# Latent attention: four reciprocals of a head become one, and the four scalings wait once

## What is computed

```python
kv_lat = xn @ W_kvd
q_lat = xn @ W_qd
k = (kv_lat @ W_ku).reshape(B, S, NH, HH)
q = (q_lat @ W_qu).reshape(B, S, NH, HH)
v = (kv_lat @ W_vu).reshape(B, S, NH, HD)
...
scores = jnp.einsum('bqhd,bkhd->bhqk', qq, kk) * scale
causal = jnp.tril(jnp.ones((S, S), dtype=bool))
scores = jnp.where(causal[None, None], scores, jnp.finfo(scores.dtype).min)
probs = jax.nn.softmax(scores, axis=-1)
y = jnp.einsum('bhqk,bkhd->bqhd', probs, v).reshape(B, S, H)
return y @ W_o
```

## Time and profile before

| what | us |
|---|---|
| median of 3 runs | 2147.19 |
| the three runs | 2139.01 to 2148.48 |
| the profiled execution | 2150.66 |
| its span, first to last instruction | 2148.7 |
| TensorE busy | 1624.5 (76%) |
| VectorE busy | 1142.2 (53%) |
| ScalarE busy | 543.6 (25%) |
| GpSimd busy | 537.0 (25%) |
| mean granted TensorE clock | 0.884 |

### The profile page before, as it was taken

The page is one execution under the profiler, slowest core; times in us unless marked ns, Lnnn a source line. Parts: engine busy times, 40 slices in busy tenths (PEclk is TensorE's granted clock), DMA queues, the critical chain, the costliest instruction groups (busy, mean ns, idle before and its releaser), DMA issues. The chain is left out here.

```text
span 2148.7 us, 34575 instructions
## 1 busy us (share of the span) xinstructions
PE 1624.5 (76%) x10302; PEld 1283.0 (60%) x10302; DVE 1142.2 (53%) x2756; ACT 543.6 (25%) x1372; POOL 537.0 (25%) x763
## 2 busy tenths in 40 slices
PE   3994999998169776877774887527898698499980
PEld 2873888887159733444442576515565486398980
DVE  5774222221866667777764223365787676422223
ACT  1441011010144323666631100022221344011100
POOL 1002111111610013667722133240222100222215
PEclk8996999999589988999996989955999799699995
DMA  3103889886300017534201288720000000599973
GB/s 114 33 0 114 299 294 305 296 297 212 89 1 0 0 61 135 79 55 63 39 1 54 70 239 264 215 67 1 0 0 0 0 0 0 170 320 305 324 254 117
DMA packets 182251, 262.65 MB, mean 122 GB/s; under 512 B 17616, under 2 KB 132752, under 8 KB 180144
## 3 DMA queue, kind: packets, MB, share of 16 engines
q1 hardware_dynamic: 171968, 234.01, 36.3%
q0 software_dynamic: 10224, 27.93, 5.0%
HBM read 231.86 MB, written 30.02 MB: 122 GB/s over the span
## 5 line engine op out<-in xcount | busy, mean ns | idle before, releaser
L1026 POOL TENSOR_TENSOR xn<-xn,l1a_rc 128x512 f32<-128x512 f32 (+3 forms) x256 | 176.1, 719 | 92.2 <-DVE l1a_rc L958 92.2
L988 ACT ACTIVATE xn<-l1a_sc,l1a_nm 128x512 f32<-128x512 f32 (+3 forms) x256 | 131.4, 525 | 88.2 <-DVE l1a_nm L952 88.2
L1081 PE MATMUL l1a_tp<-consts,xn 128*128 128x128 f32 x640 | 87.5, 287 | 45.1 <-POOL xn L1026 22.5
L1622 PE MATMUL e0b_gp<-e0b_xT,e0b_wgu 128*128 128x128 f32 x936 | 117.2, 283 | 2.5 <-DVE e0b_hT L1691 1.3
L1622 PEld LDWEIGHTS e0b_gp<-e0b_xT,e0b_wgu 128*128 128x128 f32 x936 | 109.8, 195 | 15.4 <-issue 12.3
L1206 POOL DMA_INDIRECT e_got<-y_slots,e_slot x96 | 99.9, 1041 | 75.3 <-issue 73.0
L1643 PE MATMUL e0b_yp<-e0b_wd,e0b_hT 128*128 128x256 f32 x468 | 115.1, 388 | 0.6 <-issue 0.6
L952 DVE TENSOR_REDUCE l1a_nm<-l1a_sc 128x1 f32<-128x512 f32 (+3 forms) x256 | 107.1, 480 | 4.6 <-PE l1a_sc L1069 4.4
L1672 ACT ACTIVATE e0b_sg<-e0b_gp 128x640 f32<-128x640 f32 x78 | 33.5, 481 | 286.8 <-PE e0b_gp L1622 286.8
L1081 PEld LDWEIGHTS l1a_tp<-consts,xn 128*128 128x128 f32 x640 | 73.7, 147 | 52.3 <-POOL xn L1026 51.4
L536 PE MATMUL a_sc<-a_kd,a_qT 128*128 (+2 forms) x256 | 99.5, 523 | 4.4 <-ACT a_qT L609 2.9
(11 more groups left out here) (477 smaller groups left out, 3551.3 us busy)
## 6 DMA issues: line engine op xcount, KB each, us to landing
e3b_wgu<-in_L_ffn_W SPq DMA_DIRECT2D x78, 512.0 KB
e0b_wgu<-in_L_ffn_gate_proj SPq DMA_DIRECT2D x39, 704.0 KB
e0b_wgu<-in_L_ffn_up_proj SPq DMA_DIRECT2D x39, 704.0 KB
e0b_wd<-in_L_ffn_down_proj SPq DMA_DIRECT2D x39, 640.0 KB
e3b_wd<-in_L_ffn_W SPq DMA_DIRECT2D x39, 512.0 KB
e1b_wgu<-in_L_ffn_Wg_r SPq DMA_DIRECT2D x39, 256.0 KB
e1b_wgu<-in_L_ffn_Wu_r SPq DMA_DIRECT2D x39, 256.0 KB
e1b_wd<-in_L_ffn_Wd_r SPq DMA_DIRECT2D x39, 256.0 KB
```

The lines of the kernel that those rows point to most:

```text
L988: nc.scalar.activation(pr[:, j, of_query[q]], sc[q][:, 0:(q + 1) * P], ACT.Exp, bias=nm[:, q:q + 1], accum_out=sums[:, j, q:q + 1]).then_i ...
L1026: nc.gpsimd.tensor_tensor(of, of, bcast(rc[:, j, q:q + 1], 2, (q + 1) * P), ALU.mult)\
L1081: last = nc.tensor.transpose(tp[g][:, q - k + (TB - 2 if k == TB - 1 else 0), :], pr[:, j, at:at + P], ident)
L1622: last = nc.tensor.matmul(dst[:, f, :], wgu[j][:, k, at + f * P:at + (f + 1) * P], xT[j][:, k, :], start=(k == 0), stop=(k == KC - 1))
```

## The change

`invert` becomes one instruction: it waits until the last of the head's four exponentials is done and takes the reciprocals of all four columns of sums, 128x4, at once. It adds 1 to `rec_done` in place of four times 1. `scale` waits once, for the head's reciprocal, and then issues the same four multiplications in the same order, which still add 1 to `scaled` each. Nothing else differs.

```diff
@@ -953,9 +953,8 @@
                         def invert(n, j):
-                            for m, q in enumerate(reversed(range(TB))):
-                                dve.wait_ge(exp_done, n * TB + m + 1)
-                                nc.vector.reciprocal(rc[:, j, q:q + 1], sums[:, j, q:q + 1]).then_inc(rec_done, 1)
+                            dve.wait_ge(exp_done, n * TB + TB)
+                            nc.vector.reciprocal(rc[:, j, :], sums[:, j, :]).then_inc(rec_done, 1)
@@ -1020,8 +1019,8 @@
                         def scale(n, j):
-                            for m, q in enumerate(reversed(range(TB))):
-                                pool.wait_ge(rec_done, n * TB + m + 1)
+                            pool.wait_ge(rec_done, n + 1)
+                            for q in reversed(range(TB)):
                                 of = pr[:, j, of_query[q]].unsqueeze(1)
                                 nc.gpsimd.tensor_tensor(of, of, bcast(rc[:, j, q:q + 1], 2, (q + 1) * P), ALU.mult)\
                                     .then_inc(scaled, 1)
```

## The result

| | before | changed |
|---|---|---|
| median, us | 2144.74 (9 runs) | 2156.61 (9 runs) |
| lowest to highest | 2135.27 to 2148.48 | 2151.32 to 2168.22 |
| ratio to before | 1 | 1.0071, 95% interval 1.0047 to 1.0095 |
| span of the profiled execution | 2148.7 | 2165.9 |

What follows compares the result with a forecast made beforehand. The prediction took a VectorE-ScalarE loop without slack as the bound. Terms 12.0 + 0.3 + 0.9 + 0.8 + 0.3 = 14.3 us on the 2147.19 median gave 2161.5, forecast as 2161 us (chance 0.63), range 2151 to 2170.

Steps and rivals of the forecast that it cites:

- The ring: In the 64-head attention, VectorE and ScalarE wait on each other in a loop without slack, 3.94 us a head.
- a place of no slack every fourth head: On TensorE, value products follow the turn and delay the next scores; 15 places where a later turn costs time.
- The last scaling gates the turn: TensorE's turn of a head's ten blocks would wait for GpSimd's last scaling and end 0.86 us later (0.79 to 0.99).
- The longer reciprocal: On VectorE, 128x4 takes 0.018 us more ahead of the copies in 48 heads, 0.9 us in all (0 to 4.4).
- three instructions fewer: On VectorE, removing three reciprocals a head gains nothing, as they ran in gaps ended by waits for ScalarE.
- The last head: At the attention's end, the last value products start at 1098.58 in place of 1097.75, costing 0.8 us.
- The first head: At the attention's start, it fills an empty pipeline and can lose 0 to 0.86 us; 0.3 taken.
- The place at a low clock: One of 15 places before value products, TensorE's granted clock 0.69, turn 2.23 us; cost taken as 0.3 us (0 to 0.86).
- The sum: All losses in the attention stage together: 12.0 + 0.3 + 0.9 + 0.8 + 0.3 = 14.3 us.
- the first rival: GpSimd's later scalings don't gate TensorE's turn: 4.5 to 9.4 us slower, 2152 to 2157, some 2155 us; chance 0.20.
- The ring didn't shorten: Rival: the VectorE-ScalarE loop shortens once the small reciprocals are gone, so the kernel isn't slower, 2145 us; chance 0.04.
- TensorE's clock did fall: Rival: turns broken up by waits lower TensorE's clock, four more slow value heads, 20.7 us, 2168 us; chance 0.13.

Runs made afterwards that it cites:

- plain_heads: Kernel before, with GpSimd waiting once, for the last of four reciprocals, only in the 48 heads whose turn precedes no value products; ratio to before 0.9979.
- value_heads: Kernel before, with GpSimd waiting once, for the last of four reciprocals, only in the 16 heads whose turn stands before value products; ratio to before 1.0048.
- joint_again: The changed kernel itself, unaltered, measured again in another comparison; 2156.97 us, ratio to before 1.0044.
- one_wait: Kernel before, with GpSimd waiting once in every head, for the last of the four reciprocals, which VectorE keeps; ratio to before 1.0057.
- moved_joint: Changed kernel with TensorE's value products moved behind the next head's scores; 2139.43 us, ratio to before 0.9960.
- moved_four: Kernel before, four reciprocals and four waits kept, with TensorE's value products moved behind the next head's scores; 2140.37 us, ratio to before 0.9958.

## Why the prediction was right, step by step

- **The ring sets the pace, with a place of no slack every fourth head.** Right. `plain_heads` and `value_heads` show it: the same late turn is free in 48 heads and dear in 16.
- **The last scaling gates the turn, and 0.86 us go on.** Right, and measured at 0.83, from the starts of the value products (3.32 and 2.49 us behind the last reciprocal). That the two numbers are this close is in part luck. The hand-over from GpSimd to TensorE, which no row of before bounded closer than 0.08 to 0.28, is 0.06 us where I took 0.15. Against that, the last block, which I took to be 0.27 long, has 0.33 when it runs by itself. Four heads were forecast at 17.0 us; from the first delayed maximum, 866.61, to the last, 1105.08, it is 14 times 17.03.
- **The longer reciprocal costs 0.9 us in the ring.** Wrong, it costs nothing. The 128x4 takes 178 ns, as estimated (179):

```profile
L957 DVE RECIPROCAL l1a_rc<-l1a_sums 128x4 f32<-128x4 f32 x64 | 11.4, 178 | 79.0 <-ACT xn L987 79.0
```

  But the copies start 0.10 us after its start, as after a shorter one. I had added the duration of an instruction whose end nobody in the ring waits for; the copies behind it don't need it, and what counts is start to start.
- **No gain from three instructions fewer.** Right. VectorE's busy time between the marks fell from 201.98 to 176.95 us, and the plain head stayed at 3.94. Of the two rules of the Trainium skill ("Perfetto Trace Analysis", "Optimizing Scalar/DVE Operations") the trace agrees with the second, that smaller instructions may let work be completed sooner where the engine isn't saturated: with one instruction the first scaling started 1.32 us later. The first, that grouping can raise the throughput of a saturated engine, is shown by no run here.
- **The last head, 0.8 us.** Right: from the last value head's maximum to the last value products 1111.94 - 1104.79 = 7.15 us in `joint_again`, as against 1097.75 - 1091.31 = 6.44, so 0.7. In the profiled execution of the changed kernel it is 7.76. Its last turn ran at a granted clock of 0.50 and took 2.37 us, where `joint_again` had 1.00 and 1.76 us.
- **The first head, 0.3 us.** Too much: from the first maximum to the third 845.45 - 838.28 = 7.17, as against 842.96 - 835.84 = 7.12.
- **The place at a low clock, 0.3 us.** The cost that I gave it wasn't seen. Before, this place, the fourteenth of the 15, made four heads take 1075.18 - 1057.41 = 17.77 us. The changed kernel's fourteenth place lay at the full clock and took 17.03, so its profile gains 0.7 us there. `joint_again` and `one_wait` have such a place of their own, the first, with a wait of 2.7 us.
- **The sum.** 14 x 0.83 = 11.6, with 0.7 and 0.05, is 12.4 us, where the prediction has 14.3, 0.3 of it for the place at a low clock; most of the rest is the 0.9 of the reciprocals. Between the marks the profiles show 12.65, 13.4 (`joint_again`) and 13.3 (`one_wait`). The 12.65 consists of 12.0 at 14 places, since some of them ran in part at the lower clock (waits of 1.12 to 1.16), 1.3 for the last head, 0.05 for the first, less 0.7 for the place above. Against before the two comparisons give 15 and 9 us with overlapping intervals, so these can't tell 12.4 from 14.3.
- **The time.** The median, 2156.61, is 4.4 us under the 2161 forecast, 2.45 of it because the median of before is 2144.74 over nine runs, and not the 2147.19 of three. It lies below the forecast's own bounds (2159 to 2168) and inside the 2152 to 2157 of the first rival. It is within the stated range of 2151 to 2170 only because that range took in the rivals. So the time alone couldn't have told the forecast from the first rival. What decides is the trace: the value head's wait grew from 0.20 to about 1.0 us, and the last block started after its scaling had ended.
- **Rivals.** The later scalings do gate (`one_wait`). The ring didn't shorten (3.94). TensorE's clock did fall, but it didn't add value heads that wait as long as the one at 1.79 us, four of which I had priced: each of `one_wait`, `joint_again` and `value_heads` has one such place (2.7, 2.7 and 1.9 us), as the kernel before does, and the changed kernel's profile has none.

## What to carry to other kernels

Merging small instructions saved nothing here, on an engine that waits anyway, and it delayed the first of their results to the time of the last. The price was the delay of the last consumer's input, less its slack, times the number of places that nothing covers: (1.32 - 0.49) x 14 or 15. Such places are found by asking for each consumer what stands behind it on its own in-order engine: here one turn in four had value products and then the next scores behind it. The scores didn't need what stood ahead of them, and moving them ahead of the long step was worth more than any of the reciprocals tried.

## What was not expected of the hardware

TensorE's granted clock went down with the change. The clock has two levels, 1.2 and 2.4 GHz, written 0.50 and 1.00. Over the stretch between the marks (length, busy us and instructions of PE, PEld, DVE, ACT, POOL, then the clock), for the kernel before and the changed one:

```profile
835.84:1097.75 261.91, 202.51 (x1630) 121.40 (x1629) 201.98 (x641) 171.29 (x584) 181.48 (x272) 0.96 0.41 56
```

```profile
838.28:1112.84 274.56, 220.28 (x1630) 131.96 (x1629) 176.95 (x449) 171.65 (x584) 181.85 (x272) 0.91 0.40 54
```

If all of the rest is time at 1.2 GHz, an estimate from these rows is 2 x 0.04 x 262 = 21 us at the lower level before and 2 x 0.09 x 275 = 49 us after. The other profiles have 0.90 in `one_wait` and `joint_again`, 0.94 in `value_heads`, 0.96 in `plain_heads`, `moved_joint` and `moved_four`. So the turns broken up by waits don't lower it alone, as `plain_heads` and `moved_joint` have them as well. Nor do the longer value heads: `value_heads` has them throughout, and yet over seven of them in a row its clock is the full one:

```profile
960.00:1080.00 120.00, 92.08 (x734) 50.96 (x732) 89.12 (x283) 75.94 (x260) 79.48 (x120) 1.00 0.39 53
```

The lowest values are in the kernels that have both. In the changed kernel the lower level shows mostly in plain heads. Of the four heads from 934.71 us, the second and third have it, and the first and the fourth, the value head, have 1.00:

```profile
938.75:942.69 3.94, 2.96 (x15) 1.70 (x16) 2.72 (x8) 2.62 (x9) 2.67 (x5) 0.87 1.02 133
942.69:946.63 3.94, 3.45 (x23) 2.71 (x20) 2.70 (x8) 2.62 (x9) 3.10 (x6) 0.70 1.02 133
946.63:951.76 5.13, 4.65 (x46) 2.49 (x47) 2.89 (x8) 2.62 (x9) 3.85 (x7) 1.00 0.79 102
```

There it costs nothing, as both plain heads keep their 3.94 us. The waits for scores in the changed kernel are 0.97 to 1.16 us at all 15 places, the three longest (1.12 to 1.16) behind value heads at 0.87 to 0.88; `one_wait`, `joint_again` and `value_heads` have one place each with 1.9 to 2.7 us. Why the clock falls in these heads was not tried.
